# Macaron block: constants between weight tiles, x and W2 loads reordered, states in float16 halves with the decay on the outputs

## The reference

```python
x = x + 0.5 * ffn(layernorm(x), W1, W2, W3)
x = x + attn(layernorm(x), ...)
x = x + 0.5 * ffn(layernorm(x), W1, W2, W3)
# ffn:  hidden = silu(x @ W1.T) * (x @ W3.T)   (2048 wide); fwht(hidden) @ W2.T
# attn: rmsnorm, ternary qkv weights, 16 heads of 32, chunks of 128 tokens:
scores = einsum('bhtd,bhsd,hts->bhts', qi, ki, mask)        # mask = decay exp(-s (t - s')), causal
intra  = einsum('bhts,bhsd->bhtd', scores, vi)
cross  = einsum('bhtd,ht,bhde->bhte', qi, lam_t, S)         # lam_t = exp(-s t)
o      = scale * (intra + cross)
kv     = einsum('bhtd,ht,bhte->bhde', ki, lam_rev, vi)      # lam_rev = exp(-s (128 - t))
S      = exp(-s 128) * S + kv                               # state, one 32x32 matrix per head
# then rmsnorm twice and a ternary projection
```

## Time and profile before

| | |
|---|---|
| median of 3 runs | 2354.49 us |
| profiled execution | 2355.63 us |
| span of its trace | 2353.9 us |
| PE busy | 2336.4 us, 99% |
| VectorE busy | 1232.0 us, 52% |
| ScalarE busy | 692.4 us, 29% |
| GpSimd busy | 149.8 us, 6% |
| mean granted TensorE clock | 0.999 |

### The profile page before, as it was taken

How to read it: one execution, slowest core, us unless ns; L and a number is a source line. 1 busy time by engine, 2 the same in 40 slices (tenths; PEclk the granted TensorE clock), 3 DMA queues, 4 the chain that set the end, 5 groups by cost and what they waited for, 6 DMA issues and landing times.

```text
span 2353.9 us, 31017 instructions
## 1 busy us (share of the span) xinstructions
PE 2336.4 (99%) x12407; PEld 1120.7 (48%) x12407; DVE 1232.0 (52%) x2211; ACT 692.4 (29%) x1164; POOL 149.8 (6%) x126
## 2 busy tenths in 40 slices
PE   8999999999999999999999999999999999999999
PEld 4444444444544454445444444445444544544444
DVE  6577555654565446546554465544664455445212
ACT  6645233222222222223223222222232213221211
POOL 0190000000000000000000000000000000000000
PEclk9999999999999999999999999999999999999999
DMA  8856622331243212422042223421432224131200
GB/s 218 229 152 175 157 86 64 89 86 50 68 77 107 72 28 82 103 75 64 28 138 51 54 81 90 99 54 28 121 68 85 50 54 99 31 87 36 65 25 19
DMA packets 299457, 196.83 MB, mean 84 GB/s; under 512 B 231600, under 2 KB 256176, under 8 KB 295472
## 3 DMA queue, kind: packets, MB, share of 16 engines
q1 hardware_dynamic: 299024, 194.31, 31.6%
q10 hardware_dynamic: 288, 0.52, 0.1%
HBM read 84.68 MB, written 54.53 MB: 59 GB/s over the span
## 4 chain that ended last, share of the span: by engine, by line
PE 94%; DVE 3%; issue 1%; ACT 1%; DMA 1%; SPq 0%; POOL 0%; DVEq 0%; ACTq 0%; POOLq 0%
PE d_bank L1437 27%; PE l_bank L1417 27%; PE g_bank L1417 26%; PE a_bank L1472 5%; PE a_bank L1532 2%; PE a_bank L1455 2%; PE a_bank L1483 1%; PE a_bank L1514 1%; PE a_bank L1519 1%; PE a_bank L1497 1%; DVE work L1146 1%; DVE work L1126 0%; DMA w1t<-kT 0%; PE a_bank L1521 0%; PE d_bank L1391 0%
## 5 line engine op out<-in xcount | busy, mean ns | idle before, releaser
L1437 PE MATMUL d_bank<-w2t,work 128*128 128x512 f16 x2940 | 671.9, 379 | 0.0
L1437 PEld LDWEIGHTS d_bank<-w2t,work 128*128 128x128 f16 x2940 | 284.7, 98 | 332.4 <-DVE work L1146 0.6
L1126 DVE SCALAR_TENSOR_TENSOR work<-l_bank,l_scale,work 128x512 f32<-128x512 f32 x256 | 191.8, 749 | 468.4 <-PE l_bank L1417 468.4
L1417 PE MATMUL g_bank<-xt,w1t 128*128 128x512 f16 x1536 | 354.1, 380 | 3.6 <-DMA w1t<-kT 3.6
L1417 PE MATMUL l_bank<-xt,w3t 128*128 128x512 f16 x1536 | 352.4, 379 | 0.0
L857 ACT ACTIVATE work<-g_bank,g_scale 128x512 f32<-128x512 f32 x256 | 175.4, 685 | 490.1 <-PE g_bank L1417 488.2
L876 ACT CAST work<-work 128x512 f16<-128x512 f32 x232 | 143.3, 618 | 562.0 <-DVE work L1126 561.1
L1417 PE MATMUL l_bank<-work,w3t 128*128 128x512 f16 x1344 | 308.4, 379 | 0.2 <-DVE work L1126 0.2
L1417 PE MATMUL g_bank<-work,w1t 128*128 128x512 f16 x1344 | 308.3, 379 | 0.0
L1417 PEld LDWEIGHTS g_bank<-xt,w1t 128*128 128x128 f16 x1536 | 148.3, 98 | 177.9 <-DMA w1t<-kT 4.6
L1417 PEld LDWEIGHTS l_bank<-xt,w3t 128*128 128x128 f16 x1536 | 148.1, 98 | 173.0 <-issue 0.2
(11 more groups left out here) (227 smaller groups left out, 1791.1 us busy)
## 6 DMA issues: line engine op xcount, KB each, us to landing
work<-parts_dram SPq DMA_DIRECT2D x192, 128.0 KB, 2.7
x_dram<-work SPq DMA_DIRECT2D x16, 1024.0 KB, 4.2
work<-x_dram SPq DMA_DIRECT2D x11, 1024.0 KB, 6.6
parts_dram<-q_parts SPq DMA_DIRECT2D x32, 256.0 KB, 2.0
parts_dram<-k_parts SPq DMA_DIRECT2D x32, 256.0 KB, 2.2
norm_dram<-cent SPq DMA_DIRECT2D x32, 256.0 KB, 2.0
w2t<-in_L_ffn_W_dram SPq DMA_DIRECT2D x30, 256.0 KB, 3.2
xin<-in_L_attn_x_dram SPq DMA_DIRECT2D x7, 1024.0 KB, 8.4
```

The source lines that it names most:

```text
L1126: nc.vector.scalar_tensor_tensor(out=hfull, in0=l_bank[:], scalar=l_scale[:, j:j + 1], in1=gate, op0=ALU.mult, op1=ALU.mult).then_inc(hful ...
L1417: ins = nc.tensor.matmul(dst[:], wt[:, wp, k, P * j:P * (j + 1)], src[:, xp, k, :], start=(k == 0 and wp == xp), stop=(k == KT - 1 and wp ...
L1437: ins = nc.tensor.matmul(d_bank[t][:], parts[:, hp, P * t:P * (t + 1)], w2t[:, j, wp, :], start=(j == 0 and hp == wp), stop=(j == HT - 1 a ...
```

## The change

- The sign matrix is no longer made at the start but in three steps "consts" between blocks 2 and 4 of the first pass; its scratch moves from `junk` to `cent`. `diag` goes.
- The first x is normalised into `first_cent` (a view of `zt`), all four tiles before the first turn, and the four turns use four banks instead of two. Scales of weight chunks 2 and 3 are made singly.
- Batch 1's x is loaded in four parts, after tiles 7, 9, 11 and 13.
- The pieces of W2 are made in the order 0, 2, 1, 3 of column chunks, the last six in slots of their own, and the pair steps 0 to 3 wait only for the pieces they read.
- The state is kept as 32 columns (each head's own 32x32 block), scaled by a constant, split in float16 halves, stored to DRAM ("statestore") and loaded back as 96 partitions per head ("statespread"), like `qs` and `ks`. kv and state move to slot `at`, ahead of score 0; pv steps go to +2, +4, +5, +6.
- The cross term is made from undecayed `qs` and these states, four float16 matmuls of 32 columns a chunk, one a head, into columns of their own; the decay of the outputs (`lam_out`) is a multiplication by VectorE when a chunk leaves its bank. Each chunk has a bank to itself. GpSimd's `qdec` goes. k's decay becomes one factor per chunk.

```diff
                     add(slots, at - 2, [("kturn", (b, g))])
-                    add(slots, at, [("score", (b, g, 0))])
-                    add(slots, at + 1, [("kv", (b, g)), ("score", (b, g, 1)), ("state", (b, g))])
-                    for c in range(TT):
-                        add(slots, at + 2 + c, [("pv", (b, g, c))] + ([("score", (b, g, c + 2))] if c < TT - 2 else []))
+                    add(slots, at, [("kv", (b, g)), ("state", (b, g)), ("score", (b, g, 0))])
+                    add(slots, at + 1, [("score", (b, g, 1)), ("statestore", (b, g))])
+                    add(slots, at + 2, [("pv", (b, g, 0)), ("score", (b, g, 2)), ("statespread", (b, g))])
+                    add(slots, at + 4, [("pv", (b, g, 1)), ("score", (b, g, 3))])
+                    add(slots, at + 5, [("pv", (b, g, 2))])
+                    add(slots, at + 6, [("pv", (b, g, 3))])
                     end = at + 2 + TT
...
-        SCALED = [slice(0, 1), slice(1, 2)] + [slice(j, j + 2) for j in range(2, HT, 2)]
+        SCALED = [slice(j, j + 1) for j in range(4)] + [slice(j, j + 2) for j in range(4, HT, 2)]
...
-            steps += [("turn", (key, 0)), ("prep", (key, 3)), ("turn", (key, 1)), ("wprep", 1), ("warm", 4)]
-            steps += [("turn", (key, t)) for t in range(2, TT)] + [("warm", 8), ("wsum", 2), ("wscale", 1), ("wprep", 2), ("wprep", 3)]
-            steps += [("wsum", 3), ("wscale", 2), ("wprep", 4)]
+            steps += [("prep", (key, 3)), ("turn", (key, 0)), ("turn", (key, 1)), ("turn", (key, 2)), ("wprep", 1)]
+            steps += [("turn", (key, 3)), ("warm", 8), ("wscale", 1), ("wprep", 2), ("wsum", 2), ("wprep", 3)]
+            steps += [("wscale", 2), ("wprep", 4)]
             own = {}
             flies = [("fly", (t, st)) for t in range(KT) for st in range(BUTTERFLIES)]
             for t in range(TT):
-                add(own, 7 + 2 * t, [("rows", (("ffn1", 1), t))])
+                add(own, 9 + 2 * t, [("rows", (("ffn1", 1), t))])
             for i, part in enumerate(norm_steps(("ffn1", 1))):
-                add(own, 14 + 2 * i, part)
+                add(own, 16 + 2 * i, part)
+            for part, at in enumerate((4, 6, 8)):
+                add(own, at, [("consts", part)])
             for j in range(HT):
                 steps += [("gate", j)]
                 if j < HT - 2:
                     steps += [("wprep", 2 * j + 5)]
...
-            splits = (14, 16, 18, 20, 21, 22, 23, 24, 25, 25, 26, 26, 27, 27, 28, 28)
+            splits = (14, 16, 17, 18, 20, 21, 22, 23, 24, 25, 25, 26, 27, 28, 29, 30)
...
+        CHUNK_ORDER = (0, 2, 1, 3)
...
-                    if arg == 5:
-                        sp.dma_start(x_next, x[1].rearrange("(t p) d -> p t d", p=P)).then_inc(x_next_loaded, 16)
+                    if arg in (7, 9, 11, 13):
+                        t = (arg - 7) // 2
+                        sp.dma_start(x_next[:, t, :], x[1, P * t:P * (t + 1), :]).then_inc(x_first[t], 16)
...
-                        b, fill = filled("score", ((ag - 1) // GROUPS, (ag - 1) % GROUPS, TT - 1))
+                        b, fill = filled("pv", ((ag - 1) // GROUPS, (ag - 1) % GROUPS, TT - 1))
...
+                elif step == "statestore":
+                    ag = arg[0] * GROUPS + arg[1]
+                    sp.wait_ge(state_lo, ag + 1)
+                    if ag >= 2:
+
+                        sp.wait_ge(state_moved, 16 * BLOCKS * (ag - 1))
+                    sp.dma_start(state_dram[ag % 2], state_parts).then_inc(state_stored, 16)
+                elif step == "statespread":
+                    ag = arg[0] * GROUPS + arg[1]
+                    sp.wait_ge(state_stored, 16 * (ag + 1))
+                    if ag:
+
+                        b, fill = filled("pv", ((ag - 1) // GROUPS, (ag - 1) % GROUPS, TT - 1))
+                        sp.wait_ge(a_ready[b], fill)
+                    for i, part in enumerate((0, 0, 1)):
+                        sp.dma_start(states[HD * i:HD * (i + 1)],
+                                     state_dram[ag % 2, :, part].rearrange("(h p) c e -> p h c e", h=HG)).then_inc(state_moved, 16)
...
+                elif step == "state":
+                    ag = arg[0] * GROUPS + arg[1]
+                    act.wait_ge(state_done, (TT - 2) * (ag + 1))
+                    if ag:
+
+                        act.wait_ge(state_stored, 16 * ag)
+                    nc.scalar.copy(state_parts[:, 0], state).then_inc(state_hi, 1)
...
+                elif step == "consts":
+
+                    if arg == 0:
+                        dve.wait_ge(pool_const, 4)
+                        link(nc.vector.tensor_tensor(bits_p, bits_p, bits_j, ALU.bitwise_and))
...
-                    nc.vector.tensor_tensor(state, a_bank[b][:, 0:(TT - 1) * P].rearrange("p (c e) -> p c e", c=TT - 1),
-                                            diag[:].rearrange("p (a e) -> p a e", a=1).to_broadcast([P, TT - 1, P]),
-                                            ALU.mult).then_inc(a_free[b], 1)
+                    products = a_bank[b][:, 0:(TT - 1) * P].rearrange("p (c h e) -> p c h e", c=TT - 1, h=HG)
+                    for h in range(HG):
+
+                        rows_h = slice(HD * h, HD * (h + 1))
+                        ins = nc.vector.tensor_scalar(state[rows_h], products[rows_h, :, h], STATE_SCALE, None, ALU.mult)
+                    ins.then_inc(a_free[b], 1)
...
+                    dve.wait_ge(state_hi, ag + 1)
+                    nc.vector.tensor_tensor(state_parts[:, 1], state, state_parts[:, 0], ALU.subtract).then_inc(state_lo, 1)
+                elif step == "pv":
                     a, g, c = arg
                     b, fill = filled(step, arg)
                     dve.wait_ge(a_ready[b], fill)
-                    nc.vector.tensor_reduce(x2[:, c - 1:c + 1, P * g:P * (g + 1)],
-                                            a_bank[b][:].rearrange("p (c a e) -> p c e a", c=2, a=2), AX.X, ALU.add
-                                            ).then_inc(a_free[b], 1)
+                    turns = a_bank[b][:].rearrange("p (r e) -> p r e", r=4)
+                    o = x2[:, c, P * g:P * (g + 1)]
+                    if c == 0:
+                        nc.vector.tensor_reduce(o, turns[:, 1:3].rearrange("p a e -> p e a"), AX.X, ALU.add).then_inc(a_free[b], 1)
+                    else:
+
+                        done = 2 * ((a * GROUPS + g) * (TT - 1) + c - 1)
+                        nc.vector.tensor_tensor(o.rearrange("p (h e) -> p h e", h=HG), turns[:, 0].rearrange("p (h e) -> p h e", h=HG),
+                                                lam_out[:, c - 1, HG * g:HG * (g + 1)].rearrange("p (h a) -> p h a", a=1)
+                                                .to_broadcast([P, HG, HD]), ALU.mult).then_inc(o_sum, 1)
+                        dve.wait_ge(o_sum, done + 1)
+                        nc.vector.tensor_tensor(o, turns[:, 1], o, ALU.add).then_inc(o_sum, 1)
+                        dve.wait_ge(o_sum, done + 2)
+                        nc.vector.tensor_tensor(o, turns[:, 2], o, ALU.add).then_inc(a_free[b], 1)
...
-                            pe.wait_ge(w2_turned[b], 16 * KT * CHUNKS // 4)
+                            pe.wait_ge(w2_turned[b], 16 * (KT if b < 2 else KT - 1))
                     elif i == 3:
 
                         pe.wait_ge(gate_ready, 2 * HT)
...
                     elif i >= 4:
 
                         pe.wait_ge(w2_final_lo, 2 * (i - 3))
+                        if i == 4:
+
+                            for b in (2, 3):
+                                pe.wait_ge(w2_turned[b], 16 * KT)
...
-                    b = USES[step, arg][0]
-                    if c % 2 == 0:
-                        take(step, arg)
-                    halves_o = a_bank[b][:, 2 * P * (c % 2):2 * P * (c % 2 + 1)].rearrange("p (a e) -> p a e", a=2)
+                    b = take(step, arg)
+                    turns = a_bank[b][:].rearrange("p (r e) -> p r e", r=4)
 
                     pe.wait_ge(sc_lo, TT * (a * GROUPS + g) + (c + 1))
-                    if c:
-
-                        if c == 1:
-                            pe.wait_ge(q_dec, a * GROUPS + (g + 1))
-                        if c >= 2:
-                            pe.wait_ge(state_done, (TT - 2) * (a * GROUPS + g) + (c - 1))
-                        nc.tensor.matmul(halves_o[:, 0, :], qdec[:, P * c:P * (c + 1)], state[:, c - 1, :],
-                                         start=(c == 2), stop=False, skip_group_check=True)
+                    if c == 1:
+                        pe.wait_ge(state_moved, 16 * BLOCKS * (a * GROUPS + (g + 1)))
                     v = values(x2)
                     for h in range(HG):
                         cols = slice(HD * h, HD * (h + 1))
-                        nc.tensor.matmul(halves_o[:, :, cols], sc[:, c % 2, 0, h, :], v[:, c, g, :, cols],
-                                         start=(c == 0 and h == 0), stop=True, skip_group_check=True)
```

(44 more changed lines are left out.)

104 lines of the change are left out of this document (55 added, 49 removed).

## The result

The changed kernel takes 2397.27 us in the median of four runs (2396.4 to 2398.61), the kernel before 2354.15 beside it: a ratio of 1.018, 95% interval 1.0168 to 1.0192. The forecast was 2339.5, in a range of 2331 to 2351.

The account below looks back on a forecast made before the run. TensorE, busy 99% of the span, was taken as the bound: matmul number and size plus few holes. 0.7+4.7+5.0+10.6-4.6-1.4 = 15.0 us saved, from 2355.6 profiled to 2340.6, or 2339.5 for the median; range 2331 to 2351.

Parts of the forecast that it names:

- 5, first group: First group of all, no down before score 1: the whole 1.85 us chain added, less another wait of 0.5: 1.4 lost.
- 6, chunks emptied singly: VectorE empties each chunk alone, some 3.2 us a group for 1.4, on an engine half idle: no cost.
- Part 6: States' way through DRAM and the rest: loads land at T+9.3, needed about T+11.6, 2.3 us spare; no cost.
- Rival C: States late for chunk 1 beside a 1 MB transfer: about 4 us in three groups, 12 us, 2351.5; chance 11%.
- Part 1: Start of the kernel: without the constants VectorE's first statistics end earlier, 0.7 us saved; constants and turns elsewhere cost nothing.
- Part 5: Ahead of score 1: a 1.85 us chain before score 0's masking makes it 0.15 us late, 4.6 us in 31 groups.
- rival D: Chain ahead of score 0 is 3.29 us, score 1 is 1.59 late in 31 groups: 49 us, 2384; chance 6%.
- Part 4: Output steps: four small matmuls (0.11 us) replace one float32 matmul (0.22), 0.11 saved 96 times: 10.6 us.
- B: Cross term: the four new matmuls cost 0.055 us each, so part 4 gives 0: 2350.1; chance 7%.
- B2: Cross term: weight loads don't hide, 0.096 us each, 0.38 for 0.22: 2365.8; chance 2%.
- Part 2: Fourth gate matmul: next x in four loads ends a 2.83 us wait and the slow clock after it, 4.7 us saved.
- Part 3: Last lin matmul of the second pass: W2 piece order and later splits end a 3.35 us wait, 5.0 us saved.

Follow-up runs that it names:

- Experiment 2: The changed kernel with the loads of the states one slot earlier, right behind their store: 2373.46 us, 23.8 less than the changed kernel.
- Experiment 1: The changed kernel with the norm of batch 1 back in its old slots (statistics at 7+2t, norm from 14): 2388.19 us, 9.1 less.
- Experiment 9: The changed kernel with the reorderings of experiments 1, 2 and 3, the new cross term of three of four heads left out: 2339.32 us.
- Experiment 10: The kernel before, with the float32 cross matmul left out of chunks 2 and 3 (64 of 96): 2339.06 us, 15.3 less.
- Experiment 7: The kernel before with only the next x in four loads, after tiles 7, 9, 11 and 13: 2352.63 us, ratio 0.9991.
- experiment 8: The kernel before with only the W2 pieces' order, later slots and shorter waits of the pair steps: 2349.43 us, ratio 0.9984.
- experiment 5: The changed kernel with the reorderings of experiments 1, 2 and 3, and score 0's low halves a step of their own after the products: 2339.71 us.
- experiment 3: The changed kernel with score 0 ahead of the state products and the recurrence: 2387.73 us, 9.5 less than the changed kernel.

## Why the prediction was wrong

By its own steps, start to start, in the profiled executions:

| step | forecast | measured |
|---|---|---|
| 1, the start | -0.7 | +0.7 |
| 1, the norm moved with it | not costed | +10.6 |
| 2, x in four loads | -4.7 | -4.7 |
| 3, W2 pieces | -5.0 | -3.7 |
| 4, cross term | -10.6 | -11.4 |
| 5, ahead of score 1, 31 groups | +4.6 | +17.9 |
| 5, ahead of score 2, block 0 | 0 | +1.7 |
| 5, first group | +1.4 | +3.3 |
| 6, states late | 0 | +24.4 |
| 6, chunks emptied singly | 0 | +1.7 |
| small waits | 0 | +0.3 |
| sum | -15.0 | +40.8 |

**Part 6 failed most.** "Queued behind that store's wait on SP are unparked tiles and norm splits, due slots later": that looks at what waits behind the states, and not at what stands in front of them. The residual steps of block 1 come between the slots +1 and +2 of a group that starts in block 0, and their step on SP waits for the residual and then issues a megabyte or two. Passes of 48 slots, batches of 78 and groups of 12 meet in such a way that this falls on four groups: batch 0 group 0, batch 2 group 3, batch 4 group 2, batch 6 group 1. These are the four waits. The prediction had the loads landed 2.3 us ahead of their use, from an issue right behind the store and 4.2 us from the first issue to the last landing. In the four groups they were issued 5.3 to 6.7 us after the store had landed, and took 4.4 to 8.3 us. Rival C named the megabyte as traffic, for three groups and 12 us, with "a like margin" of the q and k parts. It had half of the mechanism: it was four groups, 18.8 us of waits from start to start and 5.6 of slow clock, and the slow landing makes most of the waits, but only because the issue order puts the loads behind the megabytes. Experiment 2, which changes only the order, ends both.

**Part 1 failed by an edit that it passed over.** It costs the constants and the turns. The diff also moves the norm of batch 1 by two slots, which on VectorE is nothing; on SP it crosses one step, and that step issues 4 MB. Experiment 1 shows 9.1 us for it. Of the start itself, the first gate matmul came 0.69 us earlier, as forecast (15.88 for 16.57), in part by luck: the last x tile landed at 7.36, and the last statistics end at 8.05, 0.3 us earlier than before and not the forecast 0.7; the rest came from the order of the chain, put at nothing. And in the six other executions with this start the first gate matmul comes anywhere from 15.59 to 16.60. The order also cost something: the second tile, split after three turns, now lands after the first gate matmul.

**Part 5 had the mechanism and the place, and a size too small.** Its chain was 1.85 us and is 2.25. The recurrence (forecast 0.56, measured 0.57) and ScalarE (0.31, 0.31) were right. The four products were taken as 0.27 less 0.08 of overlap each; they last 0.26 each and don't overlap, 1.08 with the wait behind them, for 0.76. The low halves take 0.29 for 0.22. That is 0.40 us, and since the slack was already nil, all of it counts, 31 times (one of the 31 groups is 1.3 us late, the others 0.54 to 0.64). A chain computed to within 0.15 us of its limit is a risk of many times the number, not a cost of 0.15; rival D had the right sign, at 1.59 us a group; it was 0.58, close to the 0.63 at which D said that all gains are eaten, and 6% was too little for it.

**Part 4 was right** in mechanism and size: 0.12 us, 96 times, for 0.11. Experiments 9 and 10 price both sides of it at 0.025 and 0.22 us in their traces, so rivals B (0.055) and B2 (0.096) fall. The Trainium skill ("TensorE: Matmul & The Clock Gate", section "Back-to-back issue gap") gives some 81 ns for a pair of load and matmul at 128 columns. The trace does not agree: the pairs of the score, which have 128 columns, start 55 ns apart, and the new ones, with 32 columns, 25.

**Part 2 was right in the trace and too large for the median.** Experiment 7 gains 2.2 us of 4.7 in the median, not told from nothing. Two reasons are in the traces: 1.8 us come back in waits for VectorE, and experiments 8 and 10 show that the hole's size, and whether the slow clock follows, change between executions.

**Part 3** removed its wait, but VectorE is late at three lin steps by 0.3 to 1.1 us; experiment 8 has the same three.

With the three orders mended and ScalarE's wait covered, the change comes to the forecast's number, 2339.7 us (experiment 5), but that it is so near to 2339.5 is in part luck. Masking now costs 1.6 us more than before, where the sum allowed 6.0; the start loses 0.5 where it was to gain 0.7, the pieces of W2 give 3.7 for 5.0, and the waits behind chunks emptied singly cost 1.7, which the sum had at nothing.

## What to carry to other kernels

When a step moves in a list that several engines share, write down for each engine what it now passes, and what the steps in front of it issue: two slots that cost nothing on the computing engine put one 256 KB transpose behind 4 MB and cost 9 us, and three small loads written one slot too late cost 24. A late issue and a slow landing can each fit into the margin and together overrun it by far, so add them up for the place where they meet. Periods that don't divide alike (48, 78 and 12 slots here) make some repetitions of a pattern different from the one you look at: work out the worst, not the usual. And where a new chain has no slack left on an engine that the bound one waits for, price its error times the repetitions, or put work in its idle time, as experiment 5 does.

## What the runs showed of the hardware that I had not expected

- Small VectorE instructions on 32 partitions and 96 elements start 0.26 us apart, as long as they last (four in 1.04 us at 636.09); the 128x512 one ahead of them lasts 0.75 us, and they start 0.67 after it.
- After standing still, TensorE came back at either pace. After waits of 1.5 to 1.7 us (in the changed kernel and in experiments 8 and 10) the next twelve matmuls ran at full pace; after the 2.1 us wait on the states they did in the changed kernel's execution, and took 1.4 and 1.6 us more in experiments 1 and 3; after waits of 2.8 to 9.1 us they took 1.0 to 2.5 us more, and not the same for the same wait (5.9 us: 1.6 and 2.5 in one execution). The windows of two of them, with the granted clock third from the end:

```profile
314.40:318.90 4.50, 4.50 (x23) 1.79 (x21) 3.39 (x6) 1.01 (x2) 0.00 (x0) 0.62 0.02 6
110.30:114.30 4.00, 3.94 (x13) 1.52 (x14) 0.00 (x0) 0.00 (x0) 0.00 (x0) 0.65 0.58 211
```

- Weight loads of 96 rows between loads of 128 rows cost nothing extra: twelve pairs in 0.32 us, 0.027 a pair, start to start, as eight without them take 0.22.
- Loads of 24 KB landed after 1.5 to 3.6 us with nothing large just ahead of them (all 96 of experiment 2), and after 5.7 to 7.0 behind a 1 MB store and a 1 MB load. A 256 KB transpose took 3.7 us ahead of 4 MB of loads and 10.2 behind them.
